# Two base blocks of the third group drained as partial sums, and the weighed operands of two groups split sooner

## What is computed

```python
# B = 4, T = 1024, C = 1024; k = v = f, r = x
ek = exp(min(k, 30)); ekv = ek * v
a, b = a * decay + ekv_t, b * decay + ek_t       # scanned both ways
base = sigmoid(r) * (nf + nb - ekv + euk * v) / max(df + db - ek + euk, 1e-8)
y = base * (0.8 + 0.2 * tf)
h = silu(y @ rw1.T + rb1); logits = (h @ rw2.T + rb2)[:, :16] + gates
coeff = softmax of the top two logits, at their experts
out = y @ W.T + bias + sum over e, r of (y . A[e, r]) * coeff[e] * B[e, :, r]
return x + out
```

## Time and profile before

| | us |
|---|---|
| median of 3 runs (lowest, highest) | 647.75 (646.83, 650.06) |
| the profiled execution | 648.36 |
| its span | 646.5 |
| TensorE busy (weight loads) | 587.3, 91% (473.2, 73%) |
| VectorE busy | 495.3, 77% |
| ScalarE busy | 382.0, 59% |
| GpSimd busy | 384.1, 59% |
| mean granted clock of TensorE | 0.982 of full |

### The profile page before, as it was taken

How to read it: one execution, slowest core, us unless ns; L and a number is a source line. 1 busy time by engine, 2 the same in 40 slices (tenths; PEclk the granted TensorE clock), 3 DMA queues, 4 the chain that set the end, 5 groups by cost and what they waited for, 6 DMA issues and landing times.

```text
span 646.5 us, 6971 instructions
## 1 busy us (share of the span) xinstructions
PE 587.3 (91%) x2562; PEld 473.2 (73%) x2562; DVE 495.3 (77%) x546; ACT 382.0 (59%) x463; POOL 384.1 (59%) x205
## 2 busy tenths in 40 slices
PE   0055999989989999999999998999999999999997
PEld 0044787768867867888788876888788878888786
DVE  6999999999999999989998889996898131032202
ACT  6878999879869776778576856477364310020100
POOL 1999999989959965876657566674558210000100
PEclk9976999999999999999999998999999999999999
DMA  5434555458726821674134507374354503050112
GB/s 195 141 125 176 175 181 173 164 130 171 152 67 129 172 73 47 181 185 118 57 115 146 164 32 192 101 232 127 81 147 132 146 0 99 1 162 1 49 49 81
DMA packets 31090, 78.72 MB, mean 122 GB/s; under 512 B 4496, under 2 KB 4688, under 8 KB 31056
## 3 DMA queue, kind: packets, MB, share of 16 engines
q1 hardware_dynamic: 26304, 65.43, 31.6%
q0 software_dynamic: 4752, 12.85, 12.0%
HBM read 57.03 MB, written 29.62 MB: 134 GB/s over the span
## 4 chain that ended last, share of the span: by engine, by line
PE 61%; POOL 15%; DVE 13%; issue 6%; ACT 4%; DMA 1%; SPq 0%; POOLq 0%; DVEq 0%; ACTq 0%
PE acc L1151 19%; PE acc L1152 19%; PE acc L1153 19%; POOL mix L782 4%; POOL yr L763 3%; DVE mix L941 3%; POOL mix L757 2%; DVE mix L937 2%; POOL y_lo L792 2%; DVE mix L946 2%; PE acc L1185 1%; PE acc L1184 1%; POOL out L818 1%; DVE mix L968 1%; POOL wa_lo L733 1%
## 5 line engine op out<-in xcount | busy, mean ns | idle before, releaser
L1151 PE MATMUL acc<-y_hi,wa_hi 128*128 128x512 f32 x638 | 255.0, 400 | 45.8 <-POOL y_lo L792 41.5
L1152 PE MATMUL acc<-y_lo,wa_hi 128*128 128x512 f32 x638 | 252.0, 395 | 0.0
L1153 PE MATMUL acc<-y_hi,wa_lo 128*128 128x512 f32 x638 | 251.5, 394 | 0.0
L1151 PEld LDWEIGHTS acc<-y_hi,wa_hi 128*128 128x128 f32 x638 | 121.7, 191 | 75.7 <-POOL y_lo L792 42.9
L1153 PEld LDWEIGHTS acc<-y_hi,wa_lo 128*128 128x128 f32 x638 | 121.9, 191 | 26.2
L1152 PEld LDWEIGHTS acc<-y_lo,wa_hi 128*128 128x128 f32 x638 | 122.0, 191 | 24.6
L782 POOL TENSOR_TENSOR mix<-mix,kv 128x1024 f32<-128x1024 f32 x30 | 75.0, 2501 | 51.6 <-DVE mix L924 51.6
L792 POOL TENSOR_TENSOR y_lo<-yr,y_hi 128x1024 fp32r<-128x1024 f32 x31 | 76.1, 2456 | 33.3 <-ACT y_hi L463 33.3
L805 POOL TENSOR_TENSOR wx_lo<-xa,wx_hi 128x512 fp32r<-128x512 f32 x16 | 20.3, 1295 | 110.8 <-ACT wx_hi L551 110.8
L989 DVE SCALAR_TENSOR_TENSOR xo<-acc,bias_sb,xo 128x512 f32<-128x512 f32 x32 | 23.7, 742 | 72.7 <-PE acc L1153 72.6
L757 POOL TENSOR_TENSOR mix<-mix,kv 128x1024 f32<-128x1024 f32 x31 | 77.0, 2482 | 1.4 <-DVE mix L968 1.4
(11 more groups left out here) (138 smaller groups left out, 744.6 us busy)
## 6 DMA issues: line engine op xcount, KB each, us to landing
kv<-f_cm SPq DMA_DIRECT2D x32, 512.0 KB, 3.5
yr<-x_cm SPq DMA_DIRECT2D x32, 512.0 KB, 3.4
out<-xo SPq DMA_DIRECT2D x64, 256.0 KB, 4.1
out<-x_cm POOLq DMA_DIRECT2D x16, 512.0 KB, 7.8
xo<-x_cm SPq DMA_DIRECT2D x32, 256.0 KB, 4.0
out<-xo POOLq DMA_DIRECT2D x17, 256.0 KB, 5.7
xo<-w_base SPq DMA_DIRECT2D x4, 512.0 KB, 3.9
xa<-w_base SPq DMA_DIRECT2D x4, 512.0 KB, 4.5
```

Source lines behind the costliest of these rows:

```text
L1151: nc.tensor.matmul(out_ap, wh, yh, start=start, stop=False)
L1152: nc.tensor.matmul(out_ap, wh, yl, start=False, stop=False)
L1153: return nc.tensor.matmul(out_ap, wl, yh, start=False, stop=stop)
```

## The change

Eight edits, each quoted below. The part drain 3 goes from the end of step 3 to step 4, behind `exp_k`. Group 2 gets a second partial sum: outputs 19 and 20, channel blocks 0 and 1, in the banks of its outputs 0 and 1, which are now blocks 3 and 4; buffers, store, semaphores and accumulating DMA are doubled for it. In step 9 (group 0) ACT takes the exponential of the gap ahead of the copies and the split ahead of `exp_uk`, GpSimd the split ahead of `gate_n`, VectorE `forward` and `weigh` ahead of `ratio`, and TensorE turns after two depths of output 2 in place of four, with two depths between turn and spread and one behind. In step 16 VectorE does `p2` and `weigh(2)` ahead of `backward_den`. In step 19 ACT does `scale_end_den` ahead of `sigmoid_r`. In step 25 ACT splits group 4's operand right behind `split_hi`. `add_x_row` stands behind `p1` and the split on GpSimd. The waits on the partial sums' accumulating DMAs are changed from one to two, and SP's own is dropped.

```diff
-        parts_at = {(3, PART_CHUNK): (0, 4), (4, PART_EXP_K): (4, 5), (4, PART_END): (5, 8), (5, PART_END): (8, 10),
+        parts_at = {(3, PART_CHUNK): (0, 3), (4, PART_EXP_K): (3, 5), (4, PART_END): (5, 8), (5, PART_END): (8, 10),
                     (6, PART_CHUNK): (10, 12), (6, PART_END): (12, 13), (7, PART_EXP_K): (13, 16)}
 
-        LATE_DEPTH, LATE_SLOT, LATE = CB - 2, 2, SPLIT * CB + 3
-        LATE_NEXT = next(e for e in range(PARTS, 2 * PARTS) if e % XBUF == LATE_SLOT)
+        LATE_DEPTH, LATE_SLOTS, LATES = CB - 2, (2, 3), (SPLIT * CB + 3, SPLIT * CB + 4)
+        LATE_NEXT = [next(e for e in range(PARTS, 2 * PARTS) if e % XBUF == slot) for slot in LATE_SLOTS]
 
         def block_of(G, j):
-            return (3, 1, 2, 0, 4, 5, 6, 7)[j] if G == SPLIT else j
+            return (3, 4, 2, 0, 1, 5, 6, 7)[j] if G == SPLIT else j
 
         def base_from(G, j=0):
             if G < SPLIT:
                 return part_depth[G * CB + j]
-            return LATE_DEPTH if G * CB + j == LATE else 0
+            return LATE_DEPTH if G * CB + j in LATES else 0
...
-        weigh_at |= {(FIFTH + 1, AFTER_FWD): 4, (CB + 1, AFTER_FWD): 0, (first_step(1) + 1, AFTER_BWD_DEN): 1, (THIRD, AFTER_BWD_DEN): SPLIT, (first_step(3) + 1, AFTER_SCALE): 3}
+        weigh_at |= {(FIFTH + 1, AFTER_FWD): 4, (CB + 1, AFTER_FWD): 0, (first_step(1) + 1, AFTER_BWD_DEN): 1, (THIRD, AFTER_P2): SPLIT, (first_step(3) + 1, AFTER_SCALE): 3}
...
                 if s == THIRD - 1:
-                    sp.wait_ge(late_part_out, 1)
-                    sp.dma_start(at(out, LATE), xo[:, LATE_SLOT, :]).then_inc(late_part_stored, 16)
+                    for i in range(len(LATES)):
+                        sp.wait_ge(late_part_out, i + 1)
+                        sp.dma_start(at(out, LATES[i]), xo[:, LATE_SLOTS[i], :]).then_inc(late_part_stored[i], 16)
...
-            def drain_late_part():
-                act.wait_ge(late_part_done, 1)
-                act.wait_ge(out_added[LATE_SLOT], 16 * len(range(LATE_SLOT, PARTS, XBUF)))
-                nc.scalar.copy(xo[:, LATE_SLOT, :], acc[:, out_bank(SPLIT, 0), :]).then_inc(late_part_out, 1)
+            def drain_late_part(i):
+                slot = LATE_SLOTS[i]
+                act.wait_ge(late_part_done, i + 1)
+                act.wait_ge(out_added[slot], 16 * len(range(slot, PARTS, XBUF)))
+                nc.scalar.copy(xo[:, slot, :], acc[:, out_bank(SPLIT, i), :]).then_inc(late_part_out, 1)
...
                 if s == CB + 1:
+                    exp_gap(0)
                     copy_xa(0)
-                    exp_gap(0)
                     sigmoid_r(s)
                     copy_turned(0)
                     exps()
-                    exp_uk(s)
                     scale_end_den(s)
                     split_wx(0)
+                    exp_uk(s)
                     split_hi(s - 1)
                     scale_end_num(s)
                     exp_k(s + 1)
...
-                if s < UNITS and not routed and not late_sigmoid:
+                if s < UNITS and not routed and not late_sigmoid and s != THIRD + 3:
                     sigmoid_r(s)
                 if s < UNITS and not 0 < s < CB:
                     if s == 0:
                         act.wait_ge(recip_ready, 1)
                     scale_end_den(s)
+                if s == THIRD + 3:
+                    sigmoid_r(s)
                 drains(s, AFTER_DEN)
...
                 drains(s, AFTER_HI)
+                if routed and G == 4:
+                    split_wx(G)
                 if routed and G not in (3, 4):
...
-                if routed and G != 3:
+                if routed and G not in (3, 4):
                     split_wx(G)
...
+                    split_wx(0)
                     gate_n(s - 1)
-                    split_wx(0)
                     split_lo(s - 1)
...
-                    add_late()
+                    for i in range(len(LATES)):
+                        add_late(i)
...
-                for j in range(*x_rows_at.get(s, (0, 0))):
-                    add_x_row(j)
...
                     p1(s + 1)
                 if q == 1 and G == 3:
                     split_wx(G)
+                for j in range(*x_rows_at.get(s, (0, 0))):
+                    add_x_row(j)
...
-                if 0 < s <= UNITS:
+                if 0 < s <= UNITS and s != CB + 1:
...
                 groups_at(s, AFTER_FWD)
+                if s == CB + 1:
+                    ratio(s - 1)
...
+                if s == THIRD:
+                    p2(s)
+                    groups_at(s, AFTER_P2)
                 if s < UNITS:
                     backward_den(s)
                 groups_at(s, AFTER_BWD_DEN)
...
-                if s < UNITS:
+                if s < UNITS and s != THIRD:
                     p2(s)
-                groups_at(s, AFTER_P2)
+                    groups_at(s, AFTER_P2)
...
-            def late_part(kc):
+            def late_part(i, kc):
                 yh, yl = y_of(SPLIT, kc)
-                c = slice(ER, ER + P)
-                last = three(acc[:, out_bank(SPLIT, 0), :], wa_hi[:, kc, c], wa_lo[:, kc, c], yh, yl, kc == 0, kc == LATE_DEPTH - 1)
+                c = slice(ER + i * P, ER + (i + 1) * P)
+                last = three(acc[:, out_bank(SPLIT, i), :], wa_hi[:, kc, c], wa_lo[:, kc, c], yh, yl, kc == 0, kc == LATE_DEPTH - 1)
...
-                            for k in range(made, kc):
-                                late_part(k)
-                            for k in range(made, kc):
-                                base(G, 1, k)
-                            pe.wait_ge(late_part_out, 1)
-                            for k in range(kc):
-                                base(G, 0, k)
+                            for i in range(len(LATES)):
+                                for k in range(made, kc):
+                                    late_part(i, k)
+                            for i in range(len(LATES)):
+                                pe.wait_ge(late_part_out, i + 1)
+                                for k in range(kc):
+                                    base(G, i, k)
                         else:
                             while made < kc - LAG + 1:
-                                late_part(made)
-                                base(G, 1, made)
+                                for i in range(len(LATES)):
+                                    late_part(i, made)
                                 made += 1
...
-                ahead = {0: CB - 1, SPLIT: CB - 1, 4: 2}.get(G, k2)
+                ahead = {0: CB - 3, SPLIT: CB - 1, 4: 2}.get(G, k2)
+                turned_by = min(ahead + (2 if G == 0 else 3), CB)
                 if ahead > k2:
                     pe.wait_ge(xa_copied, 2 * G + 1)
                     for kc in range(k2, ahead):
@@ -1399,10 +1412,10 @@
                     pe.wait_ge(constants_ready, 2)
                 turn(G)
                 pe.wait_ge(xa_copied, 2 * G + 2)
-                for kc in range(ahead, min(ahead + 3, CB)):
+                for kc in range(ahead, turned_by):
                     base(G, 2, kc)
                 spread(G)
-                for kc in range(min(ahead + 3, CB), CB):
+                for kc in range(turned_by, CB):
```

42 lines of the change are left out of this document (21 added, 21 removed).

## The result

| | before | after |
|---|---|---|
| median, us (lowest, highest) | 647.83 (646.26, 650.16), 20 runs | 650.95 (648.85, 653.34), 20 runs |
| ratio to before, 95% interval | | 1.0046 (1.0035 to 1.0056) |
| the profiled execution / its span | 648.36 / 646.5 | 651.0 / 649.2 |
| TensorE busy | 587.3, 91% | 586.0, 90% |
| mean granted clock | 0.982 | 0.983 |

A forecast was written before the change was run, and what follows sets the result against it. TensorE's work plus its waits was taken to bound the kernel. +3.4 at the fourth turn, -4.05 in the fifth group and +0.75 at its banks summed to +0.1, giving a median of 647.9 us; range 643.5 to 651.0.

The forecast's parts named there:

- the chain: Waits followed from engine to engine through all groups: +0.1 us in sum, median 647.9, chance 0.46.
- The second turn soaks up the first group's gain: Second group's turn: routing comes at a fixed place, so none of 2.2 us survives; TensorE waits about 2.9.
- VectorE is later for GpSimd: First group: GpSimd's gate of unit 8 behind the subtractions delays its products; VectorE +0.65 from unit 11 on.
- The third group's lateness: Third group: 18 more matmuls before the last unit make the router's sums late; VectorE +2.05.
- Step 19: Fourth group: sigmoid of unit 19 behind the scaling removes a wait of 2.48 from VectorE; only 0.1 gained.
- The fifth group: Earlier split shortens TensorE's wait to 0.5 and keeps its clock up, -4.05; the next banks cost +0.75.
- the leave: Fourth group's turn: TensorE leaves it +3.4 later than before, in step with VectorE's lateness.
- The part drain's 0.46: Steps 3 and 4: with the drain behind unit 5's exponential, VectorE's wait for ScalarE goes, -0.46.
- Step 16: Third group: product before the weighing, backward scan behind it; VectorE idles about 0.9, TensorE's operand about 0.4 sooner.
- The hidden sum's wait: Third group: VectorE's wait for ScalarE before the hidden sum grows from 0.94 to about 3.
- rival C: Longer waits at the second turn and fourth group bring TensorE to 1.2 GHz: +2.65, 650.6 us, chance 0.12.
- the sum's last step: Whole kernel: the profiled run's 648.36 goes to 648.5; the median, 0.6 below it, gives 647.9.

The follow-up runs named there:

- the first group's kernel: The kernel before with the first group's edits on ScalarE, GpSimd and VectorE alone; 649.83 us, 1.0032 of before.
- zero: The kernel before with the fifth group's edits alone (ScalarE's split earlier, GpSimd's accumulating store of x behind the product); 644.87 us, 0.9954 of before.
- two late sums: The kernel before with the third group's two late partial sums and no other edit; 650.75 us, 1.0054 of before.
- the two fills of after: The changed kernel with 11 thrown-away matmuls in the second turn's wait, 648.11 us; the changed kernel with real matmuls of output 2 ahead of two turns, 648.65 us.
- step 19: The changed kernel with the sigmoid ahead of the scaling again, as in before; 650.30 us, 1.0043 of before.
- part drain and step 19: The kernel before with the part drain moved, the sigmoid moved behind the scaling, and the fifth group's split and store edits; 645.77 us, 0.9974 of before.

## What held of the prediction, and the step that failed

The median is inside the range, by 0.05, and that is luck: the chain, with 0.46 the likeliest, had no change, and the mechanism that made the kernel slower had a chance of 0.12.

**Right, with its size.** The second turn soaks up the first group's gain (wait 2.91, forecast 2.9). VectorE is later for GpSimd: +0.49 from unit 11 on in the first group's kernel against zero (+0.65), the experts at 137.82 (138.3). The third group's lateness: 1.9 with two late sums (2.05). Step 19: 0.0 (0.1). The fifth group: 3.1 gained (4.05 - 0.75 = 3.3). Without the clock the chain holds as far as two traces can tell: in the changed kernel's the fourth turn came 4.16 later than in before's, of which 1.45 is the slow second spread. That leaves 2.7, or 3.6 if both are counted from their first router matmul; 3.4 was forecast for the leave.

**Wrong, small.** The part drain's 0.46 was in one execution only: no such wait stands in the other five traces with the old place. The end of unit 20's exponential was worked out with 1.07, and its row has 1.04; and the chances put 0.32 outside the range where the text before them says about 0.2. Neither changes the forecast. Step 16 cost 0.5, not 0.9. The hidden sum's wait rose to 1.69 and not to 3, since 1.1 of the lateness came earlier, at ScalarE's exponential. Where I counted that 0.8 inside the 2.05, the two add up, at nearly the same sum.

**The step that failed** is the choice between the chain and rival C. Its price was right: 6 matmuls and the spread at 1.2 GHz gave 1.45 and 1.54 in the changed kernel's trace, where 2.65 were forecast for the two. Its 650.6 against 650.95 is closer than that earns, since it takes both falls as certain. Its condition was wrong: "a wait of 2.96 was followed by matmuls at 1.2 GHz, one of 2.03 was not" was read as a boundary between two lengths, with a chance of 0.12 that the new waits lie beyond. The traces show chances and no boundary: the waits of 2.03 to 2.05 for the first group's operand kept the clock in three traces and lost it in three. A wait of 2.9 had 2 in 3 to cost 1.45, and the change made three waits of over 2 us out of one of 2.96 and one of 2.03. The chain should have carried these as expected costs: by the counts above, about 2/3 of 1.45 and 0.6 of 1.54, together +1.9. A second slip stands in the sum's last step. The profiled execution of before had paid the fifth group's fall in full, and the -4.05 gave it back in full; the 0.6 taken off to come to the median is in part that same fall, absent in other runs. From the profiled execution the chain gives 648.5, and with the expected falls 650.4 (an estimate). The 0.6 left to the median stays open; the wait of 2.27 at the fourth group's first bank, which kept its clock in this trace and lost it in three others (2.23 to 2.25, the two fills of after and step 19), may have its share. The fastest run, 648.85, is where the chain without falls lies, and the record of the granted clocks bears that out: the three fastest runs of the changed kernel (648.85 to 649.24) are at 0.987 to 0.989 and none of the other 17 is above 0.986. Which falls each run had, only a profiled execution shows, so this stays an inference. The rule of the Trainium skill that the prediction quoted (TensorE: Matmul & The Clock Gate, "What's actually happening"), inactivity halves the clock, agrees in direction with every fall from 62 us on: each stands within or behind a wait of over 1.1 us.

**The same for before.** Its median probably holds the fall in some of its runs. Removing the wait took 1.77 by the wait and 1.33 where the clock fell, and narrowed the runs from 3.7 to 0.8 us.

Open: where 1.4 us of the 2.8 come from that filling the second turn's wait gave, and the spread of the runs with part drain and step 19.

## What to carry to other kernels

A wait of 2 us on TensorE is a price in some executions and none in others, so the same trace row at 1.00 proves nothing: count over several traces, and read the spread of the runs. It shrank to 0.8 and 0.9 us in two kernels in which the wait of 2.96 was gone or filled, but stayed at 3.0 in a third, so a wide spread is a hint and no proof. Move gained time past a hand-over only if something later is waiting for TensorE; here a group that got 2.6 us earlier only waited longer, and paid for it in clock. A drain that waits for TensorE holds everything behind it on its engine: giving ScalarE a second one cost 1.1 us before the sums themselves were late.

## What the runs showed of the hardware

The clock's fall differs between executions, in six kernels with nearly the same code up to there: waits of 2.03 to 2.05 us at the same matmul were followed by 1.00, 1.00, 1.00, 0.66, 0.52 and 0.52 of full speed. Behind 1.19 to 1.20 it fell once in eight. A fall cost 1.3 to 1.5 us where the next hand-over was waiting for TensorE, and 0.3 where TensorE had 0.5 to 0.6 to spare. Eleven matmuls without use, 2.5 us of TensorE's time, made a kernel 1.24 us faster. And the first router matmul of group 0 starts between 125.31 and 126.31 in the six traces whose code is the same up to there, which is the least that a shift between two single traces must exceed.
